# Second attention of a gated cross-attention block: probabilities with the keys on the partitions, behind a pass for the row maxima

## The reference, cut to what matters

```python
x = x + tanh(g_xattn[0]) * attention0(layernorm(x), ctx)       # one head of 512
x = x + tanh(g_ffn[0])   * ternary_ffn(layernorm(x))           # gelu, weights in {-1, 0, 1}
x = x + tanh(g_xattn[1]) * attention1(layernorm(x), ctx, mask) # 16 heads of 32
x = x + tanh(g_ffn[1])   * nvfp4_ffn(layernorm(x))             # silu, 4-bit quantised

# attention1, per batch row and head:
q = h @ Wq + bq;  k, v = split(ctx @ Wkv + bkv)
scores = where(mask, -inf, (q @ k.T) * 32 ** -0.5)   # tokens x 77
out = softmax(scores) @ v
out = concat(out over heads) @ Wout + bout
```

## Time and profile before

| | |
|---|---|
| runs | 1690.54 us median of 3 (1690.09 to 1691.76) |
| profiled execution | 1690.24 us, span 1688.4 us |
| PE, DVE busy | 80%, 80% of the span |
| ACT, POOL busy | 42%, 18% |
| mean granted TensorE clock | 0.906 of full speed |

### The profile page before, as it was taken

How to read it: one execution, slowest core, us unless ns; L and a number is a source line. 1 busy time by engine, 2 the same in 40 slices (tenths; PEclk the granted TensorE clock), 3 DMA queues, 4 the chain that set the end, 5 groups by cost and what they waited for, 6 DMA issues and landing times.

```text
span 1688.4 us, 22446 instructions
## 1 busy us (share of the span) xinstructions
PE 1346.8 (80%) x8120; PEld 696.9 (41%) x8120; DVE 1351.9 (80%) x2332; ACT 702.4 (42%) x2113; POOL 297.7 (18%) x237
## 2 busy tenths in 40 slices
PE   5053645889988998889889988898889988898775
PEld 4021213634464345434554446344634464334421
DVE  6998587868787788877887788778877887786786
ACT  2222303752276316651565247523653265515510
POOL 1102201032003201140113110321033012301000
PEclk9557867999999999999999999999989999998987
DMA  9264684034112231033103420341132311231012
GB/s 347 95 224 143 132 208 115 2 59 75 54 26 49 52 81 31 12 66 71 54 14 63 75 63 14 63 76 50 26 57 44 88 26 31 49 72 26 20 19 63
DMA packets 267429, 119.71 MB, mean 71 GB/s; under 512 B 244122, under 2 KB 244634, under 8 KB 265782
## 3 DMA queue, kind: packets, MB, share of 16 engines
q1 hardware_dynamic: 259158, 102.54, 26.9%
q10 hardware_dynamic: 8160, 15.73, 2.6%
HBM read 49.04 MB, written 8.39 MB: 34 GB/s over the span
## 4 chain that ended last, share of the span: by engine, by line
PE 43%; DVE 30%; issue 4%; ACT 3%; POOL 1%; DMA 1%; DVEq 0%; POOLq 0%; ACTq 0%
PE bank L1183 23%; PE bank L1283 8%; PE bank L1268 7%; DVE stats L735 2%; DVE hid L893 2%; DVE xt L772 2%; DVE amax L888 2%; PE bank L1373 2%; DVE region L992 2%; DVE hid L941 2%; DVE xb L918 2%; DVE pair L897 1%; PE bank L1316 1%; DVE pair L905 1%; DVE region L766 1%
## 5 line engine op out<-in xcount | busy, mean ns | idle before, releaser
L1268 PE MATMUL bank<-w_up,xt 128*128 128x512 fp8e4 x1024 | 249.1, 396 | 38.2 <-ACT region L521 34.3
L1283 PE MATMUL bank<-w_dn,region 128*128 128x512 fp8e4 x1024 | 236.3, 385 | 29.9 <-DMA region<-region 29.9
L443 POOL TENSOR_TENSOR region<-g,region 128x512 f16<-128x512 f32 x128 | 160.8, 1259 | 268.9 <-ACT region L521 260.8
L536 ACT ACTIVATE th<-bank,each 128x512 f32<-128x512 f32 x100 | 68.7, 687 | 329.8 <-PE bank L1183 321.8
L1268 PEld LDWEIGHTS bank<-w_up,xt 128*128 128x128 f16 x1024 | 103.2, 102 | 169.0 <-ACT region L521 35.3
L1183 PE MATMUL bank<-w_gate,xqt 128*128 128x512 bf16 x512 | 141.2, 401 | 36.0 <-DVE th L930 21.6
L554 ACT ACTIVATE region<-bank,nm 128x77 f32<-128x77 f32 x512 | 159.1, 336 | 21.0 <-DVE nm L973 19.8
L1283 PEld LDWEIGHTS bank<-w_dn,region 128*128 128x128 f16 x1024 | 101.4, 99 | 155.6 <-DMA region<-region 30.9
L1183 PE MATMUL bank<-w_gup,xqt 128*128 128x512 bf16 x512 | 139.6, 397 | 26.4 <-DVE hid L941 21.1
L518 ACT ACTIVATE g<-bank 128x512 f32<-128x512 f32 x128 | 76.4, 597 | 183.1 <-PE bank L1268 165.9
L1223 PE MATMUL bank<-ident,region 128*128 128x128 f32 x384 | 59.3, 305 | 81.8 <-DVE region L766 76.4
(11 more groups left out here) (211 smaller groups left out, 2575.9 us busy)
## 6 DMA issues: line engine op xcount, KB each, us to landing
out_x<-x ACTq DMA_DIRECT2D x16, 512.0 KB, 2.8
xin<-in_x ACTq DMA_DIRECT2D x14, 512.0 KB, 4.8
region<-in_w_up_t SPq DMA_DIRECT2D x1, 4096.0 KB, 14.2
hid<-in_gate_w SPq DMA_DIRECT2D x4, 1024.0 KB, 5.3
x<-in_gate_w SPq DMA_DIRECT2D x4, 1024.0 KB, 5.6
hid<-in_up_w SPq DMA_DIRECT2D x4, 1024.0 KB, 5.3
x<-in_up_w SPq DMA_DIRECT2D x4, 1024.0 KB, 5.9
hid<-in_down_w SPq DMA_DIRECT2D x4, 1024.0 KB, 4.8
```

What stands on the lines that cost most here:

```text
L443: eng.tensor_tensor(hn[1][:, t % 2, ns], g32[:, s % 2, :], hn[0][:, t % 2, ns], ALU.subtract).then_inc(sg["hl"], 1)
L536: eng.activation(th[:, u % 2, :], bank[4][:, :], ACT.Silu, scale=cg[:, :]).then_inc(sg["th"], 1)
L1268: last = mm(bank[s % 2][:, :], xt[i][:, k, ts], w_up[:, k, n * D:(n + 1) * D], start=(k == 0 and i == 0), stop=(k == KD - 1 and i == 1))
L1283: last = mm(bank[2 + t % 2][:, :], ht[i][:, t % 2, f, :], w_dn[:, f, :], start=(f == 0 and i == 0), stop=(f == KF - 1 and i == 1))
```

## The change

The second attention of a group is laid out anew. The queries are kept as eight tiles (`qt`): in each, the partitions of two heads hold their high half, and the other 64 partitions the low half of the same two heads, so that one product takes both halves. The keys stand twice on the partitions to match (ACT copies them once, at the start).

A first pass makes scores with tokens on the partitions for the maxima alone (a mask product and four products of 154 columns, now in one bank); DVE takes the maxima; at the end of a tile PE turns its 16 maxima into a row per head (`turn_max`), ACT and DVE make two halves of them (`mx`). A second pass (`shifted_scores`) makes scores with the 77 keys on the partitions, 128 tokens to a head, twelve products of 128 columns a unit; one of the three for each head subtracts the maximum. ACT takes the exponential of the whole unit twice, in float32 and as the high half (`powers_of`), POOL the low half (`low3`). The values have a column of ones behind each head, so that the same twelve products as before also give the sums (`weigh`); DVE divides, half a tile at a time. The four turns per unit, ACT's sums and the copy of the turned tile are gone.

The units run through a longer pipeline (`LAG_S` to `LAG_X3`), so later parts of each tile come three steps later; `VAR4_AT` goes from 17 to 20 and `STEPS` from 26 to 28. One of the four tiles that phase A turns for the first network is now turned behind the first up unit. The queries' low halves go from POOL to DVE, POOL's low halves of the up units 0 to 7 go from phase B into phase A's steps, and `root4` stands where the new order has it.

```diff
-VAR4_AT = TILES * NC + 1
-X4_STEPS = {VAR4_AT + 2: (0, 1), VAR4_AT + 3: (2,), VAR4_AT + 4: (3,), VAR4_AT + 5: (4,)}
-STEPS = max(TILES * NC + 10, T2_AT + 1 + UPS_A)
+LAG_MX, LAG_S = 1, 5
+LAG_V = LAG_S + 2
+LAG_ON, LAG_OT, LAG_OTL, LAG_OUT, LAG_X3 = (LAG_V + i for i in (1, 2, 3, 4, 5))
+VAR4_AT = NC + NC - 1 + LAG_X3 + 1
+X4_STEPS = {VAR4_AT + 1: (0, 1), VAR4_AT + 2: (2,), VAR4_AT + 3: (3,), VAR4_AT + 4: (4,)}
+STEPS = TILES * NC + LAG_X3
...
 # POOL
+            def low3(g, m):
+                want(pool, "p3", g, m + 1)
+                eng.tensor_tensor(pt3[1][0:M, m % 2, :], p32[0:M, m % 2, :], pt3[0][0:M, m % 2, :],
+                                  ALU.subtract).then_inc(sg["p3l"], 1)
...
             def phase_a(g3, g1):
-                if g1 is not None:
-                    root1(g1, 1)
-                    want(pool, "var2", g1)
-                    eng.tensor_tensor(sdev[:, :, :], ve2[:, :, :], powers[:, :, :], ALU.pow).then_inc(sg["rstd2"], 1)
-                if g3 is not None:
-                    root4(g3, 0)
+                for n in range(STEPS):
+                    if g1 is not None and n == max(STATS1_AT):
+                        root1(g1, 1)
+                    if g1 is not None and n == VAR2_AT:
+                        want(pool, "var2", g1)
+                        eng.tensor_tensor(sdev[:, :, :], ve2[:, :, :], powers[:, :, :], ALU.pow).then_inc(sg["rstd2"], 1)
+                    if g3 is not None and 0 <= n - LAG_S < TILES * NC:
+                        low3(g3, n - LAG_S)
+                    if g3 is not None and n == VAR4_AT:
+                        root4(g3, 0)
+                    if g1 is not None and n in UP_AT:
+                        low(g1, UP_AT[n])
...
-                for c in range(NC):
-                    want(pool, "qh", g, c + 1)
-                    eng.tensor_tensor(qt[1][:, c, :], q32[:, c % 2, :], qt[0][:, c, :],
-                                      ALU.subtract).then_inc(sg["ql"], 1)
...
 # ACT
+            def powers_of(g, m):
+                b = m // NC // 2
+                want(act, "s3", g, m + 1)
+                if m >= 2:
+                    want(act, "p3l", g, m - 1)
+                eng.activation(p32[0:M, m % 2, :], bank[6 + m % 2][0:M, :], ACT.Exp, bias=mcol[:, b:b + 1])
+                if m >= 2:
+                    want(act, "o3", g, m - 1)
+                eng.activation(pt3[0][0:M, m % 2, :], bank[6 + m % 2][0:M, :], ACT.Exp,
+                               bias=mcol[:, b:b + 1]).then_inc(sg["p3"], 1)
...
 # DVE
             def attend(g, n):
...
-                if 3 <= n <= TILES * NC + 2:
-                    m = n - 3
-                    want(dve, "p3h", g, m + 1)
-                    eng.tensor_tensor(pt3[1][0:M, m % 2], bank[6 + m % 2][0:M, :].rearrange("p (h t) -> p h t", h=HC),
-                                      pt3[0][0:M, m % 2], ALU.subtract).then_inc(sg["p3l"], 1)
...
+                    if SLOT_Q < s <= SLOT_Q + NC:
+                        c = s - SLOT_Q - 1
+                        want(dve, "qh", g, c + 1)
+                        for i in range(2):
+                            here, there = PAIR_ROWS[i], PAIR_ROWS[1 - i]
+                            eng.tensor_tensor(qt[there, 2 * c + i, :], q32[here, c % 2, :], qt[here, 2 * c + i, :],
+                                              ALU.subtract).then_inc(sg["ql"], 1)
...
 # PE
+            def shifted_scores(g, m):
...
+                for j in range(HC):
+                    h = HC * c + j
+                    q = qt[:, 2 * c + j // 2, t * P:(t + 1) * P]
+                    last = product(bank[6 + m % 2][0:M, j * P:(j + 1) * P],
+                                   [(keys1[:, 0, h, b * M:(b + 1) * M], q), (keys1[:, 1, h, b * M:(b + 1) * M], q),
+                                    (sel[0:MXR, h:h + 1].to_broadcast([MXR, M]), mx[0:MXR, t % 2, :])])
+                last.then_inc(sg["s3"], 1)
...
             def attend(g, n):
+                t = tile_at(n, LAG_MX)
+                if t is not None:
+                    turn_max(g, t)
                 if 2 <= n < TILES * NC:
                     scores(g, n)
...
+                if 0 <= n - LAG_S < TILES * NC:
+                    shifted_scores(g, n - LAG_S)
+                if 0 <= n - LAG_V < TILES * NC:
+                    weigh(g, n - LAG_V)
```

304 lines of the change are left out of this document (168 added, 136 removed).

## The result

The changed kernel takes 1816.27 us, the median of 4 runs (1807.88 to 1821.63), against 1690.32 before (1681.33 to 1691.76). The ratio is 1.0764, with a 95% interval of 1.0704 to 1.0824: slower, as forecast, but by 126 us where 58 were forecast, and outside the forecast's 1694 to 1772. It was the fastest of the four runs, 8.4 us under their median. First the busy row of the page, which answers to the earlier trace rows.

A forecast was written before the change was run, and what follows sets the result against it. It took the kernel as bound by waits between PE and DVE, with PE bounding the middle and phase B. Terms 34.8 + 4 + 4 + 14.9 = +57.7 us on 1690.24 gave 1748, range 1694 to 1772 for 8 in 10.

The forecast's parts named there:

- The unit: One attention unit on PE: twelve products of 128 columns in 0.65 us, 1.34 in all against 1.28, nothing gained.
- First phases: Before the groups, once: POOL's late reduction starts DVE's weight scaling at 150.7 instead of 135.82, +14.9 us, counted whole.
- Rival 1: The weights' delay vanishes in DVE's 27 us of waits after the first phases: 1733 us; chance 0.12.
- Query slots: Query slots and a group's start: later first row maxima and DVE's added subtractions delay the awaited low half, +2.0 us.
- Middle steps: Middle of each group: the longer pipeline removes PE's waits, leaving 20.4 of 22.5 us, so -2.1.
- Tail: End of each group's attention: five table loads instead of one and a later POOL root delay the second gate product, +5.9 us.
- Phase B: The rest of each group behind the tail: PE at 94% as before, change 0.
- Group sum: Each group in the loop: 2.0 - 2.1 + 5.9 = +5.8 us, six times, 34.8.
- First group: The first group has no quantising in its query slots, so it costs +4 us.
- Last group: The last group has no up units and so no table loads among them, so it costs +4 us.
- The rival that POOL slows DVE: Sixteen `low3` a group run beside DVE and lengthen some passes by 0.76: +17 us over seven groups, 1765; chance 0.10.
- A drain at each load: At ACT's table loads: about 1.38 us of drain per switch, 39 us more, 1785; chance 0.04.

The follow-up runs named there:

- a lag of four steps: Changed kernel with three orders mended and extra products, its second pass four steps behind the first instead of five: 1775.6 us, ratio 1.054.
- the query slots in another order: Changed kernel, second unit's scores in their own bank, first row maxima before third bank's low halves, fourth bank's after the first tile's: 1816.2 us, ratio 1.0793.

## Why the prediction was wrong, step by step

- **The unit** was right: twelve products in 0.69 us against 0.65. The rival that they cost as much as 308 columns is out.
- **First phases**, +14.9: the delay was right (14.5), in part by luck: the last low half ended 1.3 us later than forecast, and the change of code took 5.81 us instead of 7.3. The part that DVE's waits absorb was set at nothing and is 4.4. Rival 1 had the mechanism, a third of it.
- **Query slots**, +2.0: the order did what was said (`row_max` behind the third bank, the last bank's passes ahead of the first tile's low half), and PE's wait grew by 2.9 as forecast. The start cost 3.2; the 0.8 that later steps were to make up is not seen in steps that came out longer.
- **Middle steps**, -2.1: the step that failed, and with it a sum that has no term for the clock. "PE's waits go entirely: 20.4" took PE's busy time at full clock. It holds in the first group, -2.5 at the same clock. From the second group on the steps follow a wait of 7.02 us, the clock is at its lower level for 8 to 17 us of them, and they are 3.2 longer on average: 5.3 us off in each of six groups, the largest term. In groups 1, 3 and 5 they take 45.9, 47.1 and 49.0 us with 8.4, 12.9 and 16.8 us at the lower level. The run with extra products in five waits gave 1.6 of the 5.3 back and left 6.2 us at the lower level, which at half clock are at most 3.1 more, an estimate.
- **Tail**, +5.9: right at full clock, 6.4 in the first group and in groups without a low stretch (37.8 - 31.4). The loads are where the forecast put them, and the tail is 2.3 shorter without them, as it said. Against the first up unit x4 comes 11.1 us later in every group (10.8 forecast); against the group's start it is some 17 late in group 5 instead of 10, as start and steps are longer too. On average the tail cost 8.5: tails with 4.8 to 7.0 us at the lower level take 40.9 to 43.1. That is more than half of those stretches, so waits behind the slower products must have grown too; this was not followed.
- **Phase B**, 0: it is 1.4 longer on average, 3.1 in group 5, for the same instructions, and back when the clock is held.
- **Group sum**: 5.8 forecast, 16.3 measured. Start 3.2 (bound by DVE), steps -2.5 and tail 6.4 (both at an equal clock, the steps in the first group alone) would make 7.1, an estimate, near the forecast. The other 9.2 go with the lower level: 17.6 us more of it per group, half of which is 8.8, an estimate. The runs show 4.0 of it directly: with extra products in both kernels 12.3 are left (189.9 - 177.6), with 9.1 us at the lower level against 3.4. How the 5.2 between divide into clock and the extra products' own time was not taken apart.
- **First group** (+4) came out at -0.6, by luck: start 0.0, steps -2.5 and tail +6.4 make the +4, but its phase B of before had 12.6 us at the lower level and took 84.8, after 3.4 and 80.3. **Last group** (+4) came out at +10.1, of which 9.9 lie ahead of the second gate product; no edit of an order moved it (171.3 to 171.9 us), and a lag of four steps took only 0.7 off (171.1 against 171.8). It has 6.7 us more at the lower level, an estimate of 3.4; the rest stays open.
- The rival that POOL slows DVE is seen in single rows (1.99 for 1.23, with the queries' low halves on POOL), not in a sum: the 2096 DVE operations that both kernels have with the same tiles, shapes and counts take 12 us less in all after the change. A drain at each load is not seen: 1315.64 and 1.28 make 1316.92, and the exponentials begin at 1316.94.
- Slips that decide nothing: 39 us on top of 1748 are 1787, not 1785; the terms named for the eighth up unit make about 140, not 141.6; and the kernel before came out between 1679.4 and 1692.4 us in later runs, so that 3.4 us cannot be told from no change.

What was missing was a rival: the profile of before already had a wait of 4.14 us at that place, with a granted clock of 0.85 in the window that holds it, and the change was forecast to lengthen just that wait by 2.9. What the clock does behind it should have had a price of its own beside its length.

## What to carry to other kernels

A wait of the matrix engine can cost its length and then a stretch at half clock: 13.7 us of it behind the 7.02 us wait here. Read the granted clock of the stage behind each wait, and give a change that lengthens one a second term. Not every low stretch costs: in the kernel before the steps were as long without theirs. Moving work to another engine need not shorten the wait behind it: with the queries' low halves on POOL instead of DVE PE still waited 7.21 us. An added pass that must be complete before the next begins makes the pipeline longer or the matrix engine wait (36.2 us at a lag of four steps), even where its products are cheap.

## What was not expected of the hardware

The same program has groups of two lengths, 195.0 and 197.5 us, in one execution (the query slots in another order), with 34.1 and 27.3 us at the lower level and the engines otherwise as busy. And work that nobody reads made both kernels faster: 30 + 7 + 6 + 12 + 18 products a group in the changed one (1816.3 to 1780.9 us), 14 + 8 + 10 in the one before (ratio 0.9956).
